# Conditioning products moved behind attention, their fold ahead of the mix, in four steps of a two-layer linear-attention kernel

## The reference, cut to what matters

```python
xn = layernorm(x);  q = xn @ Wq + bq;  k = xn @ Wk + bk;  v = xn @ Wv + bv
k = where(mask, -inf, k);  v = where(mask, 0, v)     # layer 2: -1e6 is added to k, v is multiplied
q = softmax(q, over the head's width);  k = softmax(k, over the 128 tokens)
y = q @ (k^T v)                                       # for every head
scale, shift = split(silu(cond) @ W_film + b_film)    # cond: 32 x 1024, W_film: 1024 x 1024
h = silu(layernorm(y) * (1 + scale) + shift)
x = x + h @ Wo + bo
```

## Time and profile before

| | |
|---|---|
| median of 3 runs | 869.59 us (868.79 to 870.13) |
| profiled execution | 867.99 us, span 866.2 us |
| busy: PE / DVE / ACT / POOL | 847.5 / 676.9 / 605.8 / 548.7 us |
| PE share of the span | 98% |
| granted TensorE clock, mean | 0.996 of full speed |
| chain that ended last | PE 83%, DMA 7%, DVE 3% |

### The profile page before, as it was taken

How to read it: one execution, slowest core, us unless ns; L and a number is a source line. 1 busy time by engine, 2 the same in 40 slices (tenths; PEclk the granted TensorE clock), 3 DMA queues, 4 the chain that set the end, 5 groups by cost and what they waited for, 6 DMA issues and landing times.

```text
span 866.2 us, 20035 instructions
## 1 busy us (share of the span) xinstructions
PE 847.5 (98%) x6645; PEld 720.3 (83%) x6645; DVE 676.9 (78%) x1356; ACT 605.8 (70%) x1442; POOL 548.7 (63%) x741
## 2 busy tenths in 40 slices
PE   8989999999999999999999999999999999999998
PEld 7778888888888888888877888888888888888886
DVE  6987777778788788788887887787787788777666
ACT  5477677677676776776777786777686777676665
POOL 3366766766766756765767767666666766765641
PEclk9999999999999999999999999999999999999999
DMA  9875765766766756555587655656666655656341
GB/s 307 283 229 175 224 209 189 225 203 201 202 209 202 235 190 189 177 183 174 171 233 227 196 176 178 205 179 195 182 191 199 205 178 175 201 193 196 138 157 62
DMA packets 115692, 169.81 MB, mean 196 GB/s; under 512 B 11886, under 2 KB 84966, under 8 KB 115590
## 3 DMA queue, kind: packets, MB, share of 16 engines
q1 hardware_dynamic: 114800, 167.56, 61.5%
q10 hardware_dynamic: 790, 0.98, 0.4%
HBM read 95.61 MB, written 72.88 MB: 195 GB/s over the span
## 4 chain that ended last, share of the span: by engine, by line
PE 83%; DMA 7%; DVE 3%; SPq 2%; issue 2%; POOL 2%; ACT 1%; DVEq 0%; POOLq 0%; ACTq 0%
PE PS L1111 72%; PE PS L1207 6%; PE PS L1191 3%; DMA X<-in_x 2%; DMA k_turned<-KT 1%; DMA XT<-x_turned 1%; DMA x_turned<-XS 1%; DMA QT<-qy_turned 1%; SPq L420 1%; PE PS L1281 0%; POOL XL L626 0%; DMA EK<-k_turned 0%; SPq L367 0%; DVE BNX L1470 0%; ACT XF L894 0%
## 5 line engine op out<-in xcount | busy, mean ns | idle before, releaser
L639 POOL TENSOR_TENSOR HL<-H,HH 128x512 fp32r<-128x512 f32 x60 | 77.5, 1292 | 192.0 <-ACT HH L875 191.9
L826 ACT ACTIVATE Z<-QT,FC,FA 128x128 f32<-128x128 f32 x240 | 99.0, 483 | 91.1 <-DMA QT<-qy_turned 91.1
L1111 PE MATMUL PS<-XH,WH_k 128*128 128x256 f32 x512 | 150.4, 294 | 0.9 <-DVE KN L1536 0.7
L1111 PE MATMUL PS<-XL,WH_k 128*128 128x256 f32 x512 | 145.4, 284 | 0.0
L1111 PE MATMUL PS<-XH,WL_k 128*128 128x256 f32 x512 | 145.4, 284 | 0.0
L788 ACT ACTIVATE SK<-SK,KN 128x128 f32<-128x128 f32 x256 | 98.9, 387 | 11.3 <-DVE KN L1536 11.3
L1111 PE MATMUL PS<-WH_o,HH 128*128 128x512 f32 x248 | 103.7, 418 | 2.4 <-issue 1.9
L1111 PE MATMUL PS<-WH_v,XH 128*128 128x512 f32 x256 | 100.9, 394 | 0.0
L1111 PE MATMUL PS<-WH_q,XH 128*128 128x512 f32 x256 | 100.8, 394 | 0.0
L1111 PE MATMUL PS<-WL_v,XH 128*128 128x512 f32 x256 | 100.3, 392 | 0.0
L1111 PE MATMUL PS<-WL_q,XH 128*128 128x512 f32 x256 | 99.8, 390 | 0.0
(11 more groups left out here) (169 smaller groups left out, 2106.4 us busy)
## 6 DMA issues: line engine op xcount, KB each, us to landing
qy_turned<-QS SPq DMA_DIRECT2D x60, 512.0 KB, 2.9
QT<-qy_turned SPq DMA_DIRECT2D x240, 128.0 KB, 3.0
k_turned<-KT SPq DMA_DIRECT2D x32, 512.0 KB, 3.9
EK<-k_turned SPq DMA_DIRECT2D x128, 128.0 KB, 2.8
x_turned<-XS SPq DMA_DIRECT2D x30, 512.0 KB, 2.7
XT<-x_turned SPq DMA_DIRECT2D x120, 128.0 KB, 3.5
out_x<-X SPq DMA_DIRECT2D x31, 256.0 KB, 3.3
X<-in_x SPq DMA_DIRECT2D x11, 512.0 KB, 4.7
```

What stands on the lines that cost most here:

```text
L639: eng.tensor_tensor(hl_of(o), h_of(o), hh_of(o).bitcast(F32), ALU.subtract).then_inc(pool_hl, 1)
L826: z = eng.activation(z_of(o)[:, c * P:c * P + P].rearrange("p (q n) -> p q n", q=Q), src, ACT.Identity, bias=FC[l][:, c, b:b + 1], scale=F ...
L1111: mm = eng.matmul(dst, left[a](c), right[b](c), start=(c == 0 and a + b == 0), stop=(c == C - 1 and a == 1))
```

## The change

In the four steps the PE order becomes keys, values, queries, attention, conditioning, output, fold, mix. ScalarE copies the bank after `heads` and before `values`, where it did so before `exp_k`. VectorE does its conditioning operations after `turn_keys` rather than ahead of it. Nothing is added or removed; the order on POOL and SP is the same.

```diff
@@ scalar, step(s)
                 h_high(s - 4)
-                if s in FILM_SLOTS:
-                    conditioning_sums(FILM_SLOTS.index(s))
                 exp_k(s)
                 exp_q(s - 2)
                 heads(s - 2)
+                if s in FILM_SLOTS:
+                    conditioning_sums(FILM_SLOTS.index(s))
                 values(s)
@@ tensor, step(s)
                 keys(s)
                 values(s)
+                queries(s)
+                attention(s - 2)
                 if s in FILM_SLOTS:
                     conditioning(FILM_SLOTS.index(s))
-                queries(s)
+                output(s - 4)
                 if s in FILM_SLOTS:
                     conditioning_fold(FILM_SLOTS.index(s))
-                attention(s - 2)
-                output(s - 4)
                 mix(s - 2)
@@ vector, step(s)
                 queries(s)
+                turn_keys(s)
                 if s in FILM_SLOTS:
                     conditioning(FILM_SLOTS.index(s))
-                turn_keys(s)
```

## The result

| | before | changed |
|---|---|---|
| median, 18 runs each | 869.15 us (866.72 to 873.39) | 871.02 us (869.5 to 873.75) |
| ratio | | 1.0028, 95% interval 1.0017 to 1.0039 |
| profiled execution | 867.99 us, span 866.2 us | 869.5 us, span 867.7 us |
| PE, mix of step 8 to mix of step 30 | 285.88 us | 287.84 us |
| of that, step 16 to step 25 | 117.06 us | 119.80 us |

The account below looks back on a forecast made before the run. PE's order was taken as the bound, with the RQ-to-output chain second; joint gains less a step 17 loss were summed to -0.51 us, from 869.59 to 869.1 us, range 867.7 to 870.8.

Parts of the forecast that it names:

- What bounds the kernel: PE's own order sets the end; second, a chain from RQ through DRAM, film and HL releases output two steps later.
- The sum: Step 9 gains 0.19, step 13 0.32, step 17 costs 0.28, step 21 gains 0.32; written as -0.51 us.
- PE's joints: Changed gaps between products on PE in the four steps: gain 0.32 us a step, between 0.10 and 0.37.
- x: PE's start-to-start time from attention to conditioning: 0.35 us taken, range 0.30 to 0.48.
- y: PE's time from fold to mix: 0.36 us taken, range 0.36 to 0.45.
- The prediction's open case: A PE joint without array-shape change, unseen in the trace; changed-shape joints start 0.07 us before the modelled end.
- The fold, the order on ScalarE, the shared buffer: Next step's film waits for no fold; ScalarE's later copy and earlier QT read count for nothing.
- add_x to RQ: VectorE spacing between these starts: 0.62 us as between two turns, or 0.72 by the skill's drain rule.
- Four operations take 0.87 (247.00 to 247.87): VectorE's conditioning operations in steps 17 and 21 keep this old duration behind the fold; RQ comes 0.28 us later.
- The slack: HL's spare time before output: 0.77 us in step 18, which holds, and 0.16 in step 19, giving 0.44 wait.
- Step 21: Slack behind it taken as in step 18, so its PE gain of 0.32 us is kept.
- Rival 2: VectorE's operations between fold and add_x set the pace behind all four steps: +1.1 us, 870.7 us; chance 0.15.

Follow-up runs that it names:

- e6: e1 plus a bare VectorE wait for the fold where the changed kernel has its conditioning operations; ratio 0.9995, median 868.45 us.
- e9: e5 with the last small operation, FC, also reading PSUM; layer 2 scale and shift not computed as in the reference; ratio 1.0002, median 867.89 us.
- e1: Changed kernel with VectorE's conditioning operations one step later, in their old place between queries' maximum and turned keys; ratio 0.9988, median 866.68 us.
- e10: e1 run once more, side by side with the changed kernel; ratio 0.9989, median 867.81 us.
- e4: Changed kernel with the two shift operations of steps 17 and 21 reading PSUM and SBUF; layer 2 shift not as in the reference; ratio 1.0018, median 870.24 us.
- e3: Kernel before with only VectorE's part of the change, conditioning operations behind turn_keys; ratio 1.0000, median 868.04 us.
- e7: Kernel before with the whole change in steps 9 and 13 only; ratio 1.0004, median 869.10 us.
- e5: Changed kernel with all small two-SBUF-input operations in the four steps reading PSUM and SBUF; layer 2 scale and shift not as in the reference; ratio 1.0006, median 869.26 us.
- e8: Kernel before with the whole change in steps 17 and 21 only; ratio 1.0023, median 870.63 us.

## Why the prediction was wrong

- **What bounds the kernel:** right that PE's order sets the end and that lateness of RQ is the second limit. The path was right only for step 19. The sum lets the chain by film and DMA, two steps long, use up the slack of step 18 as well; the wait there came by a shorter one, RQ, GpSimd's numbers, `norm_y`, HH, HL, with no DMA in it.
- **PE's joints:** right in kind, a little small. x is 0.28, below my lower end of 0.30, y 0.37, and mix to mix is 0.37 us shorter in all four. But the formula has no term for the joint behind the mix, which costs 0.09 more (0.90 instead of 0.81), so the net gain is 0.28 us a step in place of 0.32. Why the mix is slower behind the fold is not shown. The prediction's open case, a joint without a change of array shape, can now be read: conditioning starts 0.18 us ahead of the modelled end of attention (243.69 + 0.46 against 243.97) and the mix 0.16 ahead of that of the fold (247.89 + 0.53 against 248.26), not 0.07.
- **The fold, the order on ScalarE, the shared buffer:** right. A bare wait costs nothing (e6), and film's idle time still ends with the read of QT.
- **add_x to RQ:** 0.60 us (250.66 to 251.26), near the 0.62 of the row of two turns, not the 0.72 of a full drain.
- **The sum** is added wrongly: -0.19 - 0.32 + 0.28 - 0.32 is -0.55, not -0.51. The forecast stays at 869.0 to 869.1 us.
- **"Four operations take 0.87 (247.00 to 247.87)": this step failed.** They took 2.20 us (248.46 to 250.66). I carried a duration measured beside an idle or lightly used GpSimd to a place beside its two longest operations. Before, in step 17, the two with both inputs in SBUF ran in a time when GpSimd worked on single columns; nothing in those rows was wrong but their neighbour. RQ came at 251.26 against 250.32, while the steps ahead had gained 0.60 us by then (the mix of step 16 at 234.37 instead of 234.97): 1.54 us later in its own frame, where I had 0.28.
- **The slack** was sized well. RQ was 1.54 + 0.37 = 1.91 us late against PE, the slack 0.77, so 1.14 us should show; step 18 grew by 1.07 (12.62 to 13.69), of which 0.94 is a wait and 0.09 the joint behind the mix.
- **Step 21** was taken as costless. There too G<-G,U took 1.22 us, and PE waited 0.82 us in step 22 and 0.97 in step 23; a wait behind step 21 was one of the prediction's own signs of being wrong.
- **Rival 2** named the place, the consequence and the threshold, with 0.51 us of lateness where 1.54 were measured; for want of the cause it had 0.15.

The kernel before already showed a small sign, in step 21, on VectorE and then on GpSimd:

```profile
299.66 0.38 DVE L1675 TENSOR_TENSOR G<-G,U 128x64 f32<-128x64 f32 x1
```

```profile
299.56 1.10 POOL L646 TENSOR_SCALAR MB<-MB 128x256 f32<-128x256 int32 x1
```

The operation that takes 0.23 us in step 17 took 0.38 here, begun 0.10 us behind the start of GpSimd's mask operation. Looking at all four steps, and not at one, would have raised the question.

With 0.92 us for the four (e9) the sum is near what I wrote down: no wait in step 18, and none of the 0.44 us that I feared in step 19. The stretch from step 8 to step 30 is 284.40 us there, 1.48 less than before. The joints give 4 x 0.28 = 1.12 of this; the rest is in smaller waits elsewhere (0.17 us in step 12 instead of 0.38, none in step 30 instead of 0.53, against 0.17 and 0.30 new in steps 20 and 25) and in differences too small to be shown as waits.

Why is e9's time nevertheless 1.0002? From the mix of step 30 to that of step 40, across the change of layers, before needs 132.93 us, e9 133.36, e1 134.40, e10 133.68, and the changed kernel 132.64 and 131.98. Over all thirteen profiles this stretch takes 131.98 to 134.67 us, and not by how early a kernel comes: e4 is early and needs 132.43. That is one profile each, and no run tested it; where the last 1 us of the gain goes stays open, as does how much of the scatter at the start of the program reaches the end. So the cause is shown for PE's waits behind steps 17 and 21, and for the time as a whole only as far as these waits reach it.

The Trainium skill (SBUF — State Buffer, Who interferes with whom) states that VectorE and GpSimd share one pair of SBUF ports as an exclusive lock: a VectorE operation in a two-port mode and a GpSimd operation block each other fully, one with two SBUF inputs contends with a GpSimd operation that reads SBUF, and one with at most one SBUF input outside these modes doesn't take part. The trace agrees in size and in the choice of operations, U<-PS,VC 0.23 and G<-G,U 1.22 us beside the same GpSimd work, and e9 with 0.22 to 0.23 for all. For FC it agrees if FC runs in a two-port mode, which no run shows. By that rule the price could have been estimated beforehand from the durations: what is left of SQ and the whole of X, at most 1.05 + 1.29 = 2.34 us. For the mask operation it agrees only in part: in e3 two-input operations that began 0.34 us and more behind its start took 0.23 us, while it ran on by the profile, and only operations that began 0.07 to 0.10 us behind its start were longer, 0.37 to 0.39 us (one in the kernel before, two in e7). The port itself is not seen in a profile; what is seen are durations, neighbours and operands.

## What to carry to other kernels

When work is moved on VectorE, take its duration from the new place: look up what GpSimd runs there, and for every small operation that reads two SBUF inputs or goes from SBUF to SBUF add what is left of GpSimd's wide two-input operation. Where one of the inputs was in PSUM they kept 0.22 to 0.23 us here, so a PSUM operand helps, or a slot in which GpSimd does column work (e1). And a kernel bound by PE can gain 1.1 us in its joints and lose 3 us one and two steps later, so follow the moved engine's results to the next matmul that waits for them.

## What the runs showed of the hardware that I had not expected

- A 64-column operation of VectorE can last 1.22 us instead of 0.23. The two-input ones held by SQ or X end 0.07 to 0.09 us behind it in all profiles here, FC 0.05 us behind it (e5, e8).
- Two in a row can each be held by another one: 1.09 and 1.19 us in e8.
- A multiplication by a constant from SBUF to SBUF is held (0.98 us in e5), the same reading PSUM isn't (0.22 in e9).
- GpSimd's one-input operation on 256 columns held neither two-input operation in e3, but operations begun 0.07 to 0.10 us behind its start took 0.37 to 0.39 us in the kernel before and in e7.
- Attention and conditioning on PE, both in groups of 32 columns, follow each other 0.28 us apart from start to start, where attention and a full product took 0.39.
- The mix takes 0.90 us to the next product behind the fold and 0.81 behind the output projection.
